# A graph kernel with 3344 gather pieces: the 16th piece of 39 groups a stage moves from GpSimd to SyncE, row by row

## What is computed

```python
# layer 0, on h = relu(layernorm(x)):
xW  = einsum('nd,rde->nre', h, W_rel)             # 8 relations
agg = segment_sum(xW[src, edge_type], dst)        # gather 1
h1  = h + gelu(layernorm(agg + h @ W_self + b_conv))
x   = x + h1 + gelu(layernorm(h1) @ W1 + b1) @ W2 + b2
# layer 1, on h = relu(layernorm(x)):
xt    = h @ W.T + bias                            # 4 heads x 32
alpha = leaky_relu(alpha_src(xt)[src] + alpha_dst(xt)[dst])
out   = segment_sum(xt[src] * segment_softmax(alpha, dst), dst)   # gather 2
x     = x + out
```

## Time and profile before

| | us |
|---|---|
| Median of 2 runs | 6047.47 |
| Lowest and highest run | 6045.95, 6048.98 |
| Span of the profiled execution | 4509.7 |
| Its own time | not among the figures given; what lies around the span isn't known |
| First piece of the first gather stage starts | 217.3 |
| First piece of the second gather stage starts | 2386.2 |

### The profile page before, as it was taken

How to read it: one execution, slowest core, us unless ns; L and a number is a source line. 1 busy time by engine, 2 the same in 40 slices (tenths; PEclk the granted TensorE clock), 3 DMA queues, 4 the chain that set the end, 5 groups by cost and what they waited for, 6 DMA issues and landing times.

```text
span 4509.7 us, 47117 instructions
## 1 busy us (share of the span) xinstructions
PE 2498.0 (55%) x13797; PEld 2093.8 (46%) x13902; DVE 2470.8 (55%) x6772; ACT 962.3 (21%) x3200; POOL 3197.0 (71%) x3372
## 2 busy tenths in 40 slices
PE   7823444444444444444444666666666666666665
PEld 3423343433434333343333556555555565555555
DVE  6741333333333333333334777777777777777777
ACT  4500111111111111111122222222222222222222
POOL 1077777777777777777756777777777777777774
PEclk9966766667667666666666787777777777777777
DMA  8712222222222222222213222222222222222221
GB/s 281 273 50 53 58 62 58 62 58 60 60 58 62 58 60 60 58 62 58 60 43 107 55 57 60 57 57 60 57 60 57 58 60 57 60 57 59 58 57 44
DMA packets 170560, 314.19 MB, mean 70 GB/s; under 512 B 58980, under 2 KB 100108, under 8 KB 169615
## 3 DMA queue, kind: packets, MB, share of 16 engines
q0 software_dynamic: 107008, 222.77, 20.6%
q1 hardware_dynamic: 47810, 81.58, 5.1%
q10 hardware_dynamic: 15490, 6.87, 0.6%
HBM read 239.51 MB, written 71.49 MB: 69 GB/s over the span
## 4 chain that ended last, share of the span: by engine, by line
POOL 68%; issue 23%; PE 6%; DVE 2%; ACT 0%; DMA 0%; POOLq 0%; DVEq 0%; ACTq 0%; SPq 0%
POOL G L512 68%; PE quad L1440 1%; PE quad L1441 1%; PE bank L1440 1%; PE bank L1441 1%; PE bank L1482 0%; PE quad L1511 0%; PE quad L1517 0%; ACT A L663 0%; POOLq L111 0%; PE quad L1434 0%; PE quad L1506 0%; DMA x_res<-in_x 0%; DMA xt_table<-w_all 0%; PE bank L1434 0%
## 5 line engine op out<-in xcount | busy, mean ns | idle before, releaser
L512 POOL DMA_INDIRECT G<-rel_table,idx x1680 | 1601.5, 953 | 705.6 <-issue 511.2
L512 POOL DMA_INDIRECT G<-xt_table,idx x1664 | 1574.6, 946 | 543.8 <-issue 543.8
L1602 PEld LDWEIGHTS quad<-ident,top 128*128 128x128 f32 x3328 | 591.1, 279 | 265.6 <-issue 265.5
L1602 PE MATMUL quad<-ident,top 128*128 128x128 f32 x3328 | 607.6, 367 | 177.5 <-DVEq L1238 177.5
L1025 DVE SCALAR_TENSOR_TENSOR agg<-bank,sel,agg 128x128 f32 x208 | 63.6, 347 | 1093.0 <-PE bank L1482 1091.6
L1633 PE MATMUL bank<-M,onehot 128*128 128x132 f32 x3328 | 432.7, 284 | 149.8 <-DVE M L1287 145.4
L1482 PE MATMUL bank<-G,onehot 128*128 128x128 f32 x1664 | 271.6, 340 | 401.3 <-DMA G<-rel_table,idx 397.0
L1633 PEld LDWEIGHTS bank<-M,onehot 128*128 128x128 f32 x3328 | 398.5, 193 | 181.6 <-issue 181.6
L1482 PEld LDWEIGHTS bank<-G,onehot 128*128 128x128 f32 x1664 | 267.6, 256 | 406.0 <-issue 406.0
L1618 PE MATMUL bank<-Z,w_all 128*128 128x8 f32 x832 | 160.5, 321 | 380.3 <-issue 374.4
L768 ACT ACTIVATE M<-G,M 128x32 f32<-128x32 f32 x1664 | 363.9, 308 | 13.6 <-ACT M L763 0.4
(11 more groups left out here) (320 smaller groups left out, 3530.9 us busy)
## 6 DMA issues: line engine op xcount, KB each, us to landing
rel_table<-G SPq DMA_DIRECT2D x98, 512.0 KB, 3.1
G<-rel_table,idx POOLq DMA_INDIRECT x1680, 2.5
G<-xt_table,idx POOLq DMA_INDIRECT x1664, 7.1
xt_table<-w_all SPq DMA_DIRECT2D x25, 264.0 KB, 3.2
x_mid<-X SPq DMA_DIRECT2D x25, 256.0 KB, 2.0
out<-A SPq DMA_DIRECT2D x24, 256.0 KB
x_res<-in_x ACTq DMA_DIRECT2D x12, 448.0 KB, 5.0
x_res<-x_mid SPq DMA_DIRECT2D x3, 1792.0 KB, 15.5
```

The costliest lines, as they stand in the source:

```text
L512: g.indirect_dma_start(out=G[:, s, c, 0:width], out_offset=None, in_=table, in_offset=bass.IndirectOffsetOnAxis(ap=idx[:, s, c:c + 1], axi ...
L1602: ins = t.matmul(banks[j][:, hd * P:(hd + 1) * P], top[:, j, hd:hd + 1].to_broadcast([P, P]), ident[:, :], start=False, stop=(hd == HEADS ...
```

## The change

`SIDES` names 39 of the 104 groups: 3, 5, 8, 10, 13, 15 and so on to 98. In both stages POOL issues only 15 pieces for such a group. SP fetches the 16th: it reads four row numbers at a time from a new array `side_idx` into registers, and for each of the 128 edges issues a DMA that brings one row of the table to one partition of `side`, a tile with three buffers. SP waits with a fourth side group until the group that used the buffer is done (`agg_done`, in the second stage `tail_ready`). PE in the first stage, DVE and ACT in the second wait for or read the side buffer. The count that says a slot has landed becomes `landed_by(g)`, since groups differ. POOL makes `side_idx` at the start with two copies. The dense stores of `x_mid` and `xt_table`, and the stores of `out`, except for the last of each and those in loops, go from SP's list to ACT's.

```diff
+SIDE_C = CHUNKS - 1
+SIDES = [g for g in range(3, MAIN - 3) if g % 5 in (0, 3)]
+SIDE_BUFS = 3
+LOADED = 4
+def landed_by(g):
+
+    return 16 * sum(CHUNKS - (x in SIDES) for x in range(g % SLOTS, g + 1, SLOTS))
...
+            def side_rows(k, g, table, width):
+
+                for lo in range(0, P, LOADED):
+                    _, rows_of = nc.values_load_multi_w_load_instructions(
+                        side_idx[g:g + 1, k, lo:lo + LOADED], engines=[mybir.EngineType.SP], min_val=0, max_val=table.shape[0] - 1,
+                        skip_runtime_bounds_check_because="the transfer checks its address against the table")
+                    for p, row in enumerate(rows_of, lo):
+                        sp.dma_start(side[p:p + 1, side_of(g), 0:width], table[bass.ds(row, 1), :]).then_inc(side_ready[k][side_of(g)], 16)
+
+            sp.wait_ge(side_set, 2)
+            for j, g in enumerate(SIDES):
+                if j >= SIDE_BUFS:
+                    sp.wait_ge(agg_done, SIDES[j - SIDE_BUFS] + 1)
+                side_rows(0, g, rel_table, D)
...
-            store_quad(0, first_of(0))
-            sp.wait_ge(s_mid, 16)
-            sp.wait_ge(s_xt, 16)
-            for n in range(1, AHEAD):
-                store_quad(n, first_of(n))
+            store_quad(AHEAD - 1, first_of(AHEAD - 1))
...
-            store_out(0, first_of(0), A)
-            for n in range(1, AHEAD):
-                store_out(n, first_of(n), A)
+            for j, g in enumerate(SIDES):
+                if j >= SIDE_BUFS:
+                    sp.wait_ge(groups.tail_ready, SIDES[j - SIDE_BUFS] + 1)
+                side_rows(1, g, xt_table, XT)
+            store_out(AHEAD - 1, first_of(AHEAD - 1), A)
...
+            g.tensor_copy(side_idx[0:GROUPS, 1, :], by_chunk(src_raw, SIDE_C)).then_inc(side_set, 1)
...
+            g.tensor_copy(side_idx[0:GROUPS, 0, :], by_chunk(key_flat, SIDE_C)).then_inc(side_set, 1)
...
-                gather(rel_table, s, D, gathered[0][s])
+                gather(rel_table, s, D, gathered[0][s], SIDE_C if gr in SIDES else CHUNKS)
...
-                gather(xt_table, s, XT, gathered[1][s])
+                gather(xt_table, s, XT, gathered[1][s], SIDE_C if gr in SIDES else CHUNKS)
...
             def quad_scalar(n, lo, last, own):
 
+                if own and n:
+                    store_xt(n - 1)
                 if not last:
                     idx_of(n, 0)
...
                 if not last:
                     idx_of(n, 3)
+                    store_mid(n)
                 third_norm(n)
...
+                    own = kind is groups and c == SIDE_C and n in SIDES
+                    rows_in = side[:, side_of(n), :] if own else G[:, s, c, :]
...
+                    if s == 1 and i >= LAG:
+                        store_done(i - LAG)
...
+                if g in SIDES:
+                    dve.wait_ge(*side_landed(1, g))
+                    dve_stop(dve)
+                    v.tensor_copy(G[:, s, SIDE_C, D:XT], side[:, side_of(g), D:XT]).then_inc(side_taken, 1)
+                    dve.wait_ge(side_taken, SIDES.index(g) + 1)
...
                 for c in range(CHUNKS):
-                    ins = t.matmul(banks[5 + k][:, 0:D], picks[k][:, c, :], G[:, s, c, 0:D], start=(c == 0), stop=(c == CHUNKS - 1))
+                    rows_in = G[:, s, c, 0:D]
+                    if c == SIDE_C and g in SIDES:
+                        pe.wait_ge(*side_landed(0, g))
+                        pe_stop(pe)
+                        rows_in = side[:, side_of(g), 0:D]
+                    ins = t.matmul(banks[5 + k][:, 0:D], picks[k][:, c, :], rows_in, start=(c == 0), stop=(c == CHUNKS - 1))
```

More of the change, by code:

```diff
@@ L222, in build @@
         onehot = sb("onehot", [P, CHUNKS, P])
+        side = sb("side", [P, SIDE_BUFS, XT])
+        side_idx = sb("side_idx", [P, 2, P], i32)
         M = sb("M", [P, CHUNKS, HEADS, HD])
@@ L319, in build @@
         gathered = [[sem(f"gathered{k}_{i}") for i in range(SLOTS)] for k in range(2)]
+        side_set, side_taken = sem("side_set"), sem("side_taken")
+        side_ready = [[sem(f"side_ready{k}_{i}") for i in range(SIDE_BUFS)] for k in range(2)]
         oh_ready, agg_done, c_group = (sem(n) for n in ("oh_ready", "agg_done", "c_group"))
@@ L379, in load_rest_group, with side_of, side_landed @@
             return eng.value_load(rest[0:1, 0, bass.ds(i, 1)], min_val=0, max_val=GROUPS - 1)
+        def side_of(g):
+            return SIDES.index(g) % SIDE_BUFS
+        def side_landed(k, g):
+            return side_ready[k][side_of(g)], 16 * P * (SIDES.index(g) // SIDE_BUFS + 1)
         def load_x(eng, q):
@@ L508, in _, with gather @@
                             pattern=[[-1, P]], channel_multiplier=1).then_inc(s_pool, 1)
-            def gather(table, s, width, done):
-                for c in range(CHUNKS):
+            def gather(table, s, width, done, chunks=CHUNKS):
+                for c in range(chunks):
                     g.indirect_dma_start(out=G[:, s, c, 0:width], out_offset=None, in_=table,
@@ L689, in forward, with store_mid, store_xt @@
                     a.activation(hid[:, c % 2, :], banks[1 + c % 2][:, :], ACT.Gelu, bias=b1col[:, c:c + 1]).then_inc(up_sb, 1)
+            def store_mid(n):
+                act.wait_ge(mid_ready, n + 1)
+                act.dma_start(x_mid[:, first_of(n):first_of(n) + QUAD, :], X[:, :, :]).then_inc(s_mid, 16)
+            def store_xt(n):
+                act.wait_ge(xt_sb, n + 1)
+                act.dma_start(xt_table.rearrange("(b p) k -> p b k", p=P)[:, first_of(n):first_of(n) + QUAD, :], xt_sbuf[:, :, :]).then_inc(s_xt, 16)
             def third_norm(n):
@@ L1355, in _ @@
                 prepare(groups, c, row_of(nkey_all, gr), row_of(run_all, gr), gr % 2)
-            scores(groups, c, 0, 0, (gathered[1][0], 16 * CHUNKS))
+            scores(groups, c, 0, 0, (gathered[1][0], landed_by(0)), 0)
             assert c.n == START
@@ L1377, in round_of @@
                 if landed:
-                    scores(groups, c, (s + 1) % SLOTS, 1 - k, landed)
+                    scores(groups, c, (s + 1) % SLOTS, 1 - k, landed, gr + 1)
                 edges(groups, c, gr, s, k, (lambda: merge(groups, c, gr - 1, gr - 1, last, 1 - k)) if last is not None else (lambda: None))
@@ L1494, in _ @@
             pe.wait_ge(s_setdve, 6)
[L1495 to L1499 removed]
+            for g in range(2, LAG * SLOTS):
+                add_group(g)
             def flip(done, count):
@@ L1574, in quad_tensor @@
                 for s in range(1, SLOTS - 1):
[L1575 removed]
+                    add_group(g + s)
                 forward(n)
```

44 lines of the change are left out of this document (22 added, 22 removed).

## The result

The changed kernel takes 9131 us (median of 2 runs, 9129 to 9133), the kernel before 6047: a ratio of 1.514, 95% interval 1.496 to 1.533. The forecast of 5920 us is wrong in sign, and the time lies outside its range.

What follows compares the result with a forecast made beforehand. POOL's issue of gather pieces was taken as the bound: 6047.5 less 133.4 us (78 pieces at 1.71 us) is 5914.1, plus 6 us for first side groups and stage ends gives 5920; own range 5900 to 5990, whole range 5895 to 6870.

Steps and rivals of the forecast that it cites:

- POOL's beat is the bound: POOL's gathers in both stages: one piece starts every 1.25 us in the trace, and this issue rate bounds the kernel.
- The 1538 us lie in the gather beats, 6 in 10: POOL's gathers: run time beyond the profiled span (6047.5 against 4509.7) stretches each unprofiled beat from 1.25 to 1.71 us.
- the rival with nothing won: Excess lies in an engine with room in the profile and POOL waits for it; 6047 us, or 5980; chance 0.12.
- SP keeps up at 0.484 us a row: SP's side rows: transfer 277, register operation 48, load share 69, gaps 90 ns; 62 us a side group; chance 0.50.
- the rosier break-even of 0.52: SP's side rows: SP keeps up while a row costs under 0.52 us, from POOL's 133.4 us for five groups.
- my high bound of 0.676: SP's side rows: dearest row price, 389 + 56 + 141 + 90 = 676 ns, or 87 us a side group.
- SP the bound, at the profile's pace: Rival: excess outside, POOL's beat 1.25 us, SP's rows set the pace; 6850 us, 400 later each stage; chance 0.26.
- The rival's 7130: Variant of SP as the bound: all engines slower alike without a profile, by 1.34, giving 7130 us.
- Small parts at nothing: Index copies on POOL, moved stores on ACT, DVE's copy: hidden, no cost; without that cover some 35 us.
- "Slower": Summed chance that the changed kernel is slower: 0.26 + 0.08 = 0.34.
- the top, 6870: Upper end of the whole predicted range, just past the centre of the rival with SP as the bound.
- the dear bound of a rival: SP as the bound with rows at 676 ns: about 8760 us; half of that rival, 0.13, left outside the range.

Runs made afterwards that it cites:

- e5: Changed kernel with each side group fetched by one 128-row transfer at a fixed address instead of 128 single rows; 4407.2 us, ratio 0.9771, kernel before 4510.9.
- e10: Changed kernel with side groups one in four instead of two in five; 4448.8 us, ratio 0.9863, kernel before 4510.6.
- e15: Changed kernel with side groups three in ten and register loads of 16 instead of four; 4432.5 us, ratio 0.9829, kernel before 4508.9.
- e1: The kernel before, unedited, run beside itself; 6055.1 us, ratio 1.0015, with a profiled span of 6006.0 us.
- e3: Changed kernel with side groups one in ten, 20 pieces in all; 6056.9 us, ratio 1.0019 to the kernel before.
- e9: The changed kernel, unedited, run again where the kernel before takes 4510.6 us; 6223.9 us, ratio 1.3806.
- e2: The changed kernel, unedited, run again where the kernel before takes 6055.1 us; 9113.7 us, ratio 1.5065.
- e4: Changed kernel with no side groups, keeping the moved stores and the index copies; 6043.6 us, ratio 0.9987 to the kernel before.
- e6: Changed kernel with 128 single-row transfers per side group at fixed addresses, without register loads or register operations; 4408.3 us, ratio 0.9772.
- e16: Changed kernel with POOL fetching 8 of 16 pieces a group (7 in side groups), SP's rows kept; 6214.8 us, kernel before 4511.0.
- e17: Changed kernel without side groups, stores moved, POOL fetching 8 of 16 pieces a group; 3858.8 us, ratio 0.8554, kernel before 4511.0.

## Why the prediction was wrong

The forecast was 127 us less; the time rose by 3084. Two steps failed, on the place of the excess and on SP's row.

**POOL's beat is the bound.** Right at the quicker pace (e5, e10 and e15 get 104, 62 and 76 us for 97.5, 62.5 and 72.5), wrong at the one at which the result was measured: there the trace of e1 has POOL idle 2725 us and waiting for DVE and PE, and e3's 20 pieces are worth nothing.

**The 1538 us lie in the gather beats, 6 in 10.** This is the first step that failed. The beat is 1.25 us at both paces; the excess lies in PE's pauses beside running gathers. I saw that the median was a third over the span and explained it by stretching the one number that the forecast needed. The text had the other possibility, an engine that the profile shows with room, as the rival with nothing won, at 0.12: it was right on where the excess lies (PE), and wrong in its price, because I let SP be untouched by whatever slowed PE. My objection, that PE would have to double, looked at its busy time (2498 us, in e1 2665); what grew are the pauses between its matmuls.

**SP keeps up at 0.484 us a row.** The second step that failed, and enough for a loss by itself: even undisturbed, five groups ask for 147 us of SP, where the forecast had 133.4. Too low in two ways. Undisturbed, the row is 0.574. Term by term: the transfer 225 ns for my 277; the register operation 37 for 48; a MOVE of 29 that I left out; the load of four 563 for 277, so 141 a row for 69; what is left, mostly gaps, 574 − 225 − 37 − 29 − 141, is 142 for 90. A gap was sized rightly: in e9's trace they are 40 ns in the mean, my 40; but with the MOVE there are 3.25 a row, not 2.25. With that row even the rosier break-even of 0.52 is missed. In the Trainium skill, "DMA: Bandwidth & Descriptors", section "Latency and other measured facts", the load's floor of about 600 ns gave a row of 565: for the loads of four the trace agrees (563), and my argument that the 277 of one register decides was the wrong way round: the 562 in the earlier trace rows was the nearer of its values. Disturbed, the mean row is 0.85 to 0.88, beyond my high bound of 0.676, which knew only durations of an execution without the disturbance.

**SP the bound, at the profile's pace.** This rival had the mechanism in full. SP is solid from 216 us, PE and DVE wait for the side rows, POOL idles. It gave +800 us with 62 us a side group; with 0.574 us a row, 2 × 4992 × 0.090 = 899 us come on top, 1699 in all, and e9 measures 6207 − 4510 = 1697 between the spans. That it fits to 2 us is chance: e9's four runs spread over 23. (The rival's 7130 for all engines slower alike is by its own terms 6047.5 + 1.34 × 800 = 7120.) At the slower pace it needs the mean row measured there: SP's two stages there take 4232 and 4374 us in e2, where POOL's took 2614 and 3072 in e1, 2920 more of the 3108 between the spans.

**Small parts at nothing.** Right, as far as e4 shows it at the slower pace, where POOL's beat isn't the bound; at the quicker pace e5 leaves no room for a cost either.

**Chances and range.** "Slower" had 0.34, and the top, 6870, cut off the dear bound of a rival whose high end stood at 8760. The measured 9131 lies above that too: no number of the prediction reaches it.

## What to carry to other kernels

The gains and losses here are those of the quicker pace. Before work is moved to an idle engine, price the whole instruction sequence of one unit on it (with the loads, moves and gaps), and compare it with the time of the work that it replaces: here 73.5 us a side group against 49 us that the ring has for two and a half groups; one group in four fitted and won 1.4%, three in ten with wider loads 1.7%; two in five lost 38%. When the time and the span of the profile differ by a third, neither says what bounds the other: take from the profile no more than the usual durations for the slower execution, and give the reading "another engine is stretched there, and so may be the one that I load" its full price. What a chain promises holds only down to the next bound: halving the pieces won a third of what the beats promised.

## What the runs showed of the hardware

- The same kernel has two paces: 6057 us in the series of runs on one chip, 4509 to 4511 in the four that followed, each on another chip, steady within each. As each chip had one series, chip and time aren't told apart. At the slower, SP issues 6.3 rows in 10 us beside running gathers and 17.1 beside none; at the quicker 17.4 and 17.5. PE's matmuls of L1633 start 0.70 us apart in the mean beside running gathers, 0.18 beside none, and at the quicker pace 0.13. Instructions of POOL, DVE and ACT keep their median durations (POOL's piece 945 ns for 944, DVE's L1251 2292 for 2292, ACT's L768 307 for 307).
- A load of registers on SP takes 563 ns for four and 1255 for 16. A single-row transfer takes SP 252 ns at a fixed address (e6), and 225 with its address in a register (e9), plus 37 for a register operation and 29 for a MOVE.
- Between time and span lie 1.5 to 2 us in these runs.

What stays open: that the gathers are what slows SP and PE is read from traces, not tried, since every later run met the quicker pace. e16 and e17 at the slower pace would have tested it. Why that chip differs, what an idle stretch of 0.7 us is, and what e10 and e15 do there is not known. An estimate for e15: the mean row of 0.85 us less the 0.07 that its wider loads save at the quicker pace (0.574 to 0.50) asks for 100 us of SP a side group, in the 91 that ten thirds of a 27.4-us group give, so I would expect it to lose there.
